# Two-layer spectral and hyperbolic-norm kernel: 16 map rows stored, each loaded twice, in place of 24 stored and loaded once

## What is computed

```python
x = x + _L0_conv_ref(_gn(x), w_re, w_im, bias)   # rfft2, a 32 x 17 corner of modes mixed per head, irfft2
x = x + _L1_conv_ref(_gn(x), gamma, beta)        # the layer below, over the 64 channels of each pixel

alpha = max(xf[:, 0] * mu[0] - xf[:, 1:] @ mu[1:], 1 + EPS)     # mu: normalised mean over all pixels
d = arccosh(alpha);  var = mean(d * d)                          # over the whole batch
coef = d / sqrt(alpha * alpha - 1)
v = coef * (xf - alpha * mu);  vo = v - v[0] / (1 + mu[0]) * (mu + e0)
s = gamma * vo[1:] / (sqrt(var) + EPS) + beta;  t = sqrt(1 + sum(s * s));  out = [t, s]
```

## Time and profile before

| | us |
|---|---|
| median of 3 runs | 3578.98 |
| lowest and highest | 3571.15 and 3595.31 |
| profiled execution | 3573.87 |
| its span in the profile | 3572.3 |
| first pass | about 0 to 1010 |
| second pass (first load of x to last maps stored) | 1059 to 1930 |
| final pass | 1937 to the end |

### The profile page before, as it was taken

One profiled execution on the slowest core, in us unless ns is written; L12 is line 12 of the kernel. 1 busy time (PEld: TensorE's weight loads), 2 busy tenths in 40 slices (PEclk: granted clock), 3 DMA queues, 4 the chain that ended last, 5 costly groups with the idle time before them and its releaser, 6 DMA issues. The chain is left out here.

```text
span 3572.3 us, 69803 instructions
## 1 busy us (share of the span) xinstructions
PE 2887.4 (81%) x26018; PEld 1418.3 (40%) x26018; DVE 2648.6 (74%) x2600; ACT 2158.7 (60%) x2994; POOL 1541.4 (43%) x862
## 2 busy tenths in 40 slices
PE   6999999999617567777671898888888889888887
PEld 3555555555402122222220544444444444444443
DVE  0788888888866635645562698888888888888888
ACT  6998888888500101101110788777787778777777
POOL 0112121111211112112211688777787777777777
PEclk9999999999759788887885899999999999999999
DMA  9888797979349899999994799999999999999998
GB/s 377 298 292 315 276 329 272 330 274 326 126 149 400 314 380 407 397 389 392 400 376 98 289 383 389 368 377 382 376 379 368 374 373 367 377 369 381 378 377 338
DMA packets 293208, 1211.31 MB, mean 339 GB/s; under 512 B 35265, under 2 KB 49798, under 8 KB 210694
## 3 DMA queue, kind: packets, MB, share of 16 engines
q1 hardware_dynamic: 263526, 1152.42, 84.4%
q0 software_dynamic: 14112, 43.37, 3.7%
q10 hardware_dynamic: 15360, 12.60, 1.2%
HBM read 883.89 MB, written 324.31 MB: 338 GB/s over the span
## 5 line engine op out<-in xcount | busy, mean ns | idle before, releaser
L1297 POOL TENSOR_TENSOR c_ot<-c_ot,c_pp 128x1024 f32<-128x1024 f32 x512 | 1214.7, 2374 | 409.7 <-DVE c_ot L1250 408.5
L1240 DVE SCALAR_TENSOR_TENSOR c_xt<-c_xt,keep_k,c_p_u 128x1024 f32<-128x1024 f32 x512 | 653.8, 1277 | 124.8 <-PE c_p_u L1120 97.5
L1250 DVE SCALAR_TENSOR_TENSOR c_ot<-c_p_f,keep_k,c_xt 128x1024 f32<-128x1024 f32 x512 | 657.2, 1284 | 117.8 <-DMA out<-c_ot 69.6
L1194 ACT ACTIVATE c_pp<-c_p_p,keep_cols 128x1024 f32<-128x1024 f32 x512 | 571.2, 1116 | 262.8 <-PE c_p_p L1132 261.4
L1120 PE MATMUL c_p_u<-c_mv,c_zc 64*128 64x256 f32 x4096 | 595.0, 410 | 74.8 <-DVE c_xt L1240 73.0
L1201 ACT ACTIVATE c_sq<-c_xt,keep_cols 128x1024 f32<-128x1024 f32 x512 | 583.3, 1139 | 60.0 <-DVE c_xt L1240 59.8
L330 ACT ACTIVATE a_junk<-a_xt 128x1024 bf16<-128x1024 f32 x512 | 537.7, 1055 | 26.6 <-DMA a_xt<-in_x 19.4
L249 PE MATMUL a_p_rows<-a_xt,a_dft_h 128*64 128x512 f32 x2048 | 515.7, 647 | 36.5 <-DMA a_bias_t<-in_bias 18.5
L1120 PEld LDWEIGHTS c_p_u<-c_mv,c_zc 64*128 64x128 f32 x4096 | 361.1, 190 | 353.8 <-issue 211.2
L1132 PE MATMUL c_p_f<-c_rt,keep_lw 64*128 64x512 bf16 x1024 | 313.0, 386 | 114.1 <-DVE c_ot L1250 101.6
L516 POOL TENSOR_TENSOR a_sm<-a_sm 128x8 f32<-128x8 f32 x16 | 26.8, 1672 | 806.4 <-DVE a_sm L457 806.4
(11 more groups left out here) (205 smaller groups left out, 3032.0 us busy)
## 6 DMA issues: line engine op xcount, KB each, us to landing
a_xt<-in_x SPq DMA_DIRECT2D x256, 1024.0 KB, 8.8
b_xt<-in_x SPq DMA_DIRECT2D x128, 2048.0 KB, 16.8
c_xt<-in_x SPq DMA_DIRECT2D x256, 1024.0 KB, 16.2
out<-c_ot SPq DMA_DIRECT2D x256, 1024.0 KB, 16.5
c_rt<-maps SPq DMA_DIRECT2D x256, 96.0 KB
maps<-b_maps ACTq DMA_DIRECT2D x192, 64.0 KB, 13.5
maps<-b_maps POOLq DMA_DIRECT2D x64, 192.0 KB, 9.4
dmap<-b_dmap POOLq DMA_DIRECT2D x16, 768.0 KB, 13.5
```

The costliest lines, as they stand in the source:

```text
L1194: S.activation(pp[n][:], p_p[:], ACT.Identity, bias=keep["cols"][:, b, 1:2]).then_inc(pp_done, 1)
L1240: V.scalar_tensor_tensor(out=u, in0=u, scalar=kc, in1=p_u[:], op0=ALU.mult, op1=ALU.add).then_inc(u_done, 1)
L1250: V.scalar_tensor_tensor(out=ot[t % NB][:, at], in0=p_f[:], scalar=kinv, in1=xt[t % NB][:, at], op0=ALU.add, op1=ALU.mult).then_inc(f_done, 1)
L1297: P.tensor_tensor(o, o, pp[n][:], ALU.add).then_inc(o_done, 1)
```

## The change

The second pass makes four parts of each map in place of three: high, middle, low, and high again (a copy made by DVE, L853 of the new kernel). POOL stores all eight rows of pieces (256 KB an issue, still four issues), 16 map rows a batch. ACT's twelve issues are gone, with their semaphore `again_out` and the two waits on it. The final pass loads each of the 16 rows twice by a zero step in the source, into 32 partitions 2, 6, 10, ... of `c_rt`; of these eight copies a map, six have a weight and two meet zeros. The number of products does not change.

```diff
-MAP_AT, MAP_STEP = 4, 5
-MAP_PAIRS = ((0, 2, 4), (1, 3), (5,))
+MAP_AT, MAP_STEP = 2, 4
+MAP_SLOTS = ((0, 2, 4), (1, 3), (6,))
...
-                    m[MAP_AT + MAP_STEP * (12 * a + 2 * pair + s), at + 2 * part + s] = 1.0
+                    m[MAP_AT + MAP_STEP * (16 * a + 4 * (slot // 2) + 2 * s + slot % 2), at + 2 * part + s] = 1.0
...
-    maps_v = io["maps"].rearrange("b (q g s) (k j n) -> b g j (s k) q n", q=6, g=2, j=4, n=512)
+    maps_v = io["maps"].rearrange("b (q s) (k j n) -> b j (s k) q n", s=2, j=4, n=512)
...
-    again_out = sem("again_out")
...
-        maps = sb("maps", [128, 6, 512], BF16)
+        maps = sb("maps", [128, 8, 512], BF16)
...
-            def repeat_maps(b):
-
-                act.wait_ge(maps_ready, b + 1)
-                for j in range(4):
-                    at = slice(32 * j, 32 * j + 32)
-                    for a in (0, 3):
-                        act.dma_start(maps_v[b, 1, j, :, a:a + 2], maps[at, a:a + 2]).then_inc(again_out, 16)
-                    act.dma_start(maps_v[b, 1, j, :, 2::3], maps[at, 0::3]).then_inc(again_out, 16)
-
             def entry(b):
                 copy_z(b)
                 distances(b)
-                repeat_maps(b)
...
-            act.wait_ge(again_out, B * 192)
...
-                    pool.dma_start(maps_v[b, 0, j], maps[at]).then_inc(maps_out, 16)
+                    pool.dma_start(maps_v[b, j], maps[at]).then_inc(maps_out, 16)
...
-                    dve.wait_ge(again_out, b * 192)
...
-                both = ((coef, 0, w1), (beta, 3, w2))
+                both = ((coef, 0, w1), (beta, 4, w2))
...
+                ch.inc(V.tensor_copy(maps[:, 3::4], maps[:, 0::4]))
                 ch.inc(V.tensor_tensor(maps[:, 2], w1[:], maps[:, 1], ALU.subtract))
-                V.tensor_tensor(maps[:, 5], w2[:], maps[:, 4], ALU.subtract).then_inc(maps_ready, 1)
+                V.tensor_tensor(maps[:, 6], w2[:], maps[:, 5], ALU.subtract).then_inc(maps_ready, 1)
...
-PER_B = 15
+PER_B = 16
...
-                sp.dma_start(r[MAP_AT:MAP_AT + 24 * MAP_STEP:MAP_STEP], maps_v[b, t]).then_inc(r_in[t % NB], 16)
+                sp.dma_start(r[MAP_AT::MAP_STEP], maps_v[b, t].unsqueeze(1).to_broadcast((16, 2, TC))).then_inc(r_in[t % NB], 16)
...
-        io["maps"] = dram("maps", (B, 24, HALF), BF16)
+        io["maps"] = dram("maps", (B, 16, HALF), BF16)
```

More of the change, by code:

```diff
@@ L86, in constants @@
     for a, at in enumerate((12, 18)):
-        for part, pairs in enumerate(MAP_PAIRS):
-            for pair in pairs:
+        for part, slots in enumerate(MAP_SLOTS):
+            for slot in slots:
                 for s in range(2):
-                    m[MAP_AT + MAP_STEP * (12 * a + 2 * pair + s), at + 2 * part + s] = 1.0
+                    m[MAP_AT + MAP_STEP * (16 * a + 4 * (slot // 2) + 2 * s + slot % 2), at + 2 * part + s] = 1.0
     c["misc"] = m
```

## The result

| | before | after |
|---|---|---|
| median | 3581.63 us, 4 runs | 3757.44 us, 4 runs |
| lowest and highest | 3571.15 and 3595.31 | 3748.80 and 3766.33 |
| ratio | 1 | 1.0489, 95% interval 1.0443 to 1.0534 |
| span of the profiled execution | 3572.3 | 3751.3 |

The kernel became slower by 176 us, and nearly all of it lies in the second pass. In the new kernel the lines are 12 lower than before (L804 for L816, L855 for L867, L811 for L823), near L664 to L673 they are one lower; DVE's new copy is L853.

What follows compares the result with a forecast made beforehand. The second pass was taken as bound by DVE's wait for modes behind POOL's stores, slowed by x. Rounds of 69.0 us and the tail gave +204.5, the final pass +5: +209.5 on 3573.87, rounded to 3780; 8-in-10 range 3615 to 3840.

Steps and rivals of the forecast that it cites:

- Which wait bounds the pass: Second pass: PE's z_sb wait falls from 180.6 us to under 30; DVE waits some 38 us a round for modes.
- x beside the stores: Second pass: x's loads and the map stores start together each round, and x's filled queue slows POOL's queue to a quarter.
- The wait stretch, 40.3 us: Second pass, from maps done to the next modes' landing: 40.3 us each round, bounds 16 and 43.
- I take 2 off: Second pass, maps done to landing: 2 us less because x starts with a single tile queued and not four.
- last round's -3: Last of the fourteen second-pass rounds: 3 us less, as the x stream ends before the modes have landed.
- Landing to maps done, 28.1 + 0.6: Second pass, modes' landing to next maps done: 28.1 us as before, plus 0.6 for DVE's extra copy.
- The tail: End of the second pass: the last dense waits for the previous batch's stores, 27 us in place of 40.1, -13.
- The final pass: Final pass: loading 128 KB of maps a tile and not 96 adds 5 us, bounds 0 and 22.
- A: Whole kernel faster: bytes decide, x's next load comes over some 5 us after the stores; about -40, 3534 us; chance 0.11.
- B: Second pass: x comes two or three us after the stores, stretch about 30 us, round 58; 3631 us; chance 0.10.
- C: Whole kernel unchanged: bytes decide, but the final pass pays all 22 us and the tail gives little; 3561 us; chance 0.05.
- D: Final pass: the repeated load is cut over two engines, over 500 us more, above 4200 us; chance 0.02.

Runs made afterwards that it cites:

- first experiment: Against the changed kernel, ScalarE's copy_z(b) also waits for the maps of batch b - 1, holding PE up again; 3565.2 us, ratio 0.9974.

## Why the prediction was right, and where its sizes were off

The forecast was 3780, the measurement 3757.

**Which wait bounds the pass.** Right. Waits for `z_sb` under 30 us: 25.4. PE waiting over 20 us a batch for `b_vm`: the idle time is 255.0 / 14 = 18.2, slightly under. L804 waiting some 38 us in each round: 36.8 (515.6 / 14). DMA share near 0.75: 0.79 to 0.84. Last maps near 2120 us: 2087.2.

**x beside the stores.** Right, and the experiments carry it: hold PE, and with it x's next loads, and 192 us come back; change only the order and 150 go; take the modes out from behind the stores and x may stream. In the kernel after, the queues in 1266 to 1299, and behind them those in 1200 to 1212:

```profile
q1 hardware_dynamic: 614, 9.01, 73.5%
q0 software_dynamic: 696, 2.51, 22.4%
```

```profile
q1 hardware_dynamic: 115, 1.62, 40.4%
q0 software_dynamic: 299, 0.91, 32.1%
```

In the long stretch packets are again near equal in number, 614 and 696, while x takes three quarters of the time, and POOL's queue gets 2.51 MB in 33 us, 0.076 MB/us, as in the earlier trace rows. The rule of the Trainium skill that I weighed ("DMA: Bandwidth & Descriptors", section "Queues, rings and completion order": queues with work are served in turn, packet by packet) agrees with these counts. What it meant for POOL's queue beside x decided the sign against what the bytes said. In the 12 us from 1200, around the first stores of the round before, x moved only 1.62 MB and had 40.4% of the time; more on this below.

**The wait stretch, 40.3 us: this term was mis-sized.** It measured 38.0 on average. SP's issues of x around the maps that were done at 1265.21, and SP's and POOL's around those of 1201.20 and 1332.58:

```profile
1258.24 0.33 SPq L633 DMA_DIRECT2D b_xt<-in_x  x1
...
1267.94 0.33 SPq L633 DMA_DIRECT2D b_xt<-in_x  x1
```

```profile
1202.62 0.60 POOL L759 DMA_DIRECT2D maps<-b_maps  x1 [11.29 <-DVE b_maps L855]
...
1205.62 0.33 SPq L633 DMA_DIRECT2D b_xt<-in_x  x1
...
1333.66 0.33 SPq L633 DMA_DIRECT2D b_xt<-in_x  x1
...
1334.00 0.60 POOL L759 DMA_DIRECT2D maps<-b_maps  x1 [11.28 <-DVE b_maps L855]
```

Around 1265.21 it is as forecast: a single tile is queued when the stores come, and the next load is asked for 1267.94 - 1250.46 = 17.5 us after `combine` ended (17 forecast), 1.3 us behind the first store. But there are three kinds of rounds, by when this load of x is asked for:

| x's load against the first store | rounds | maps done to landing |
|---|---|---|
| 0.3 to 1.1 us ahead | 3 | 41.4 to 41.9 us |
| 1.3 or 1.4 us behind | 5 | 39.0 to 39.2 us |
| 3.0 us behind | 6 | 34.7 to 35.7 us |

In the 6 us from the first store POOL's queue moved 0.13 MB in the round of 1332.58, 0.38 in that of 1265.21 and 0.72 in that of 1201.20, so each us by which x comes later gives the stores a better start. PE's granted clock goes with it: in the 19 us that end 3 us after the first store it was 0.84 to 0.85 in two of the first kind, 0.76 to 0.78 in the second and 0.71 to 0.74 in the third, and a slower PE frees x's buffer later (a group of eight matmuls of L654 takes 1.93 us in the slow parts of these stretches and 1.03 in the others).

The step that failed is the size of "I take 2 off". Without it the sum is 42.3 us, and the rounds with x ahead measured 41.9; on average 4.3 would have had to come off. The 2.3 us that were missed, 14 times, are 32 of the 35 us by which the rounds were forecast too long (218.4 with the last round's -3, measured 183.0). Another 6 are 28.7 us in place of 28.3 in the rest of the round, and the -3 for the last of the fourteen rounds, which the trace doesn't show (67.5 us), goes against them.

**Landing to maps done, 28.1 + 0.6.** Measured 28.3. The copy L853 takes 0.43 us, within the bounds given, and hardly lengthens the round.

**The tail.** -13 forecast, -12.0 measured: the last `dense` waits for the stores of the batch before it, as said (L825, 12.95 us). The last stores and the passage to the final pass: -1.5 forecast, -5.2 measured.

**The final pass.** +5 forecast within 0 to 22, +13.2 measured from its clearing (0.8%). Other profiled executions agree: with 24 rows 1635 to 1639 us (the kernel before, the order alone and early modes), with 32 partitions 1645 to 1655 (after, both holds, early modes), some 11 apart. So the extra 32 KB a tile is neither free nor paid in full. SP's issue did get shorter, 546 ns in place of 758, with no effect to be seen.

**The rivals.** A, bytes decide, fell in this kernel: it asked that x come over 5 us after the stores, and x came at most 3.0 us after the first. Once the modes don't wait for the stores the change gives the sign that A says, and 14 to 18 us of the 40 it priced. B's condition, x 2 or 3 us late, was met in six of the fourteen rounds, and so was the sign that I had named for it. Its price was too low: these rounds took 34.7 to 35.7 us from maps done to landing and not 30, since POOL's queue moved 0.72 MB in the first 6 us, 0.12 MB/us, half the 0.24 that B gave it. (B's round was 28.7 + 30 = 58.7, which is 822 us for fourteen and not 812.) So my forecast of rounds near the long ones was right for eight rounds, and the other six lay between it and B. That the mix came out at 66.3 us, inside the range of 63.7 to 71.7, is in part luck. C and D are excluded by the times; D's place too, since the final pass grew by 13 us and not by 500.

## What to carry to other kernels

Before a wait is removed, ask what it keeps out of the way: here PE's stall of 180 us throttled the large stream just when the small, urgent transfers had to pass. A load that an engine will wait for should not stand in the queue behind stores that hardly anything waits for; moving it ahead was worth 217 us in the kernel after and 19 in the kernel before, and with it the change is a small gain and not a loss. The order of calls on an engine that "only copies" belongs to the sum of a change as much as what it stores.

## What the runs showed of the hardware

- A queue of small packets beside one of large ones gets a third to a half of what it gets with the other nearly empty: 0.076 MB/us beside x in the kernel after (packets of 3.6 KB beside 14.7 KB on average), 0.16 MB/us with x nearly absent (first experiment), 0.24 in the earlier trace rows.
- An engine that is held does not stop the transfers already asked for: x moved 6.55 MB in the 20 us from 1380 to 1400 while PE stood (the hold until the stores had landed).
- ACT's instructions behind its DMA issues start when these are done, and the profile shows the issues as idle time with no releaser: twelve issues took 9.3 us in the kernel with the order changed and 12.6 us in the kernel before.
- How a small load is cut into issues is worth 61 us in 256 tiles at equal bytes (1568.1 against 1629.3), while 24 to 32 rows cost 11. That the number of engines is the reason is argued.
